# Sorted tables read eight entries at a time into the registers of four engines, in a routed matmul kernel

## The reference

```python
def _L0_cond_ref(x, cat_ids, W, b):
    selected_W = W[cat_ids]          # W: [32, 512, 512]
    selected_b = b[cat_ids]          # b: [32, 512]
    return jnp.einsum('bti,bio->bto', x, selected_W) + selected_b[:, None, :]
x = x + _L0_cond_ref(x, itok_B_0_30, L0_cond_W, L0_cond_b)   # x: [128, 128, 512] f32
```

## Time and profile before

| what | value |
|---|---|
| median of three runs | 361.69 us |
| the profiled execution's own time | 361.52 us |
| its span in the trace | 359.0 us |
| TensorE busy, share of the span | 99% |
| GpSimd, VectorE, ScalarE busy | 75%, 48%, 41% |
| register loads (L146): SyncE, TensorE, VectorE, GpSimd | 64, 32, 32, 7 |

### The profile page before, as it was taken

The page is one execution under the profiler, slowest core; times in us unless marked ns, Lnnn a source line. Parts: engine busy times, 40 slices in busy tenths (PEclk is TensorE's granted clock), DMA queues, the critical chain, the costliest instruction groups (busy, mean ns, idle before and its releaser), DMA issues.

```text
span 359.0 us, 6838 instructions
## 1 busy us (share of the span) xinstructions
PE 354.1 (99%) x1553; PEld 289.6 (81%) x1553; DVE 172.9 (48%) x277; ACT 146.9 (41%) x263; POOL 269.3 (75%) x147
## 2 busy tenths in 40 slices
PE   8999999999999999999999999999999999999996
PEld 3888888888888888888888888888888888888884
DVE  7665445444544544544454454454545445445442
ACT  5464344434433443443443343342544344334420
POOL 4788999997747698799965999799979799934000
PEclk9999999999999999999999999999999999999999
DMA  7999998999788988989997899989997999855632
GB/s 267 271 403 377 394 375 289 334 361 354 284 281 276 370 325 302 307 273 392 333 306 272 287 387 322 302 306 370 332 324 267 379 371 310 315 204 179 194 117 88
DMA packets 43668, 109.49 MB, mean 305 GB/s; under 512 B 4849, under 2 KB 4850, under 8 KB 39026
## 3 DMA queue, kind: packets, MB, share of 16 engines
q1 hardware_dynamic: 38018, 69.75, 54.3%
q0 software_dynamic: 5328, 38.28, 30.9%
q10 hardware_dynamic: 288, 1.05, 0.8%
HBM read 75.50 MB, written 33.55 MB: 304 GB/s over the span
## 4 chain that ended last, share of the span: by engine, by line
PE 98%; DVE 1%; issue 0%
PE pA L411 97%; PE pA L371 1%; DVE os L364 0%; DVE cmp L318 0%; DVE below L323 0%; DVE rank L320 0%; DVE hot L321 0%; PE pS L384 0%; DVE fill L305 0%; DVE colf L316 0%; PE pS L379 0%; DVE unit L307 0%; PE pS L378 0%; DVE num L322 0%; DVE ones L306 0%
## 5 line engine op out<-in xcount | busy, mean ns | idle before, releaser
L364 DVE TENSOR_TENSOR os<-pA,bb 128x512 f32<-128x512 f32 x128 | 88.5, 691 | 171.1 <-PE pA L411 169.2
L284 ACT ACTIVATE xh<-xs 128x512 fp32r<-128x512 f32 x127 | 80.4, 633 | 195.3 <-PE pA L411 133.2
L258 POOL TENSOR_TENSOR wl<-wr,wh 128x2048 fp32r<-128x2048 f32 x30 | 138.7, 4623 | 2.5
L411 PE MATMUL pA<-wh,xh 128*128 x512 | 137.2, 389 | 0.0
L411 PE MATMUL pA<-wl,xh 128*128 x512 | 137.0, 389 | 0.0
L411 PE MATMUL pA<-wh,xl 128*128 x512 | 136.9, 389 | 0.0
L411 PEld LDWEIGHTS pA<-wh,xl 128*128 128x128 f32 x512 | 96.0, 188 | 20.2 <-DVE xl L331 0.3
L411 PEld LDWEIGHTS pA<-wl,xh 128*128 128x128 f32 x512 | 96.1, 188 | 20.0
L411 PEld LDWEIGHTS pA<-wh,xh 128*128 128x128 f32 x512 | 96.0, 188 | 20.1
L336 DVE TENSOR_TENSOR xl<-pT,xh 128x512 fp32r<-128x512 f32 x127 | 86.6, 682 | 9.9 <-ACT pT L287 9.9
L254 POOL TENSOR_SCALAR wh<-wr 128x2048 fp32r<-128x2048 f32 x30 | 57.5, 1915 | 36.7 <-PE pA L411 34.9
(11 more groups left out here) (40 smaller groups left out, 13.3 us busy)
## 6 DMA issues: line engine op xcount, KB each, us to landing
xs<-xt SPq DMA_DIRECT2D x128, 256.0 KB, 5.3
out<-os SPq DMA_DIRECT2D x128, 256.0 KB, 5.0
wr<-w POOLq DMA_DIRECT2D x29, 1024.0 KB, 7.0
bb<-bias POOLq DMA_DIRECT2D x7, 1024.0 KB, 9.6
wr<-w ACTq DMA_DIRECT2D x2, 512.0 KB, 4.3
wr<-w SPq DMA_DIRECT2D x2, 512.0 KB, 5.7
wr<-w SPq DMA_DIRECT2D x4, 256.0 KB, 7.2
bb<-bias SPq DMA_DIRECT2D x2, 256.0 KB, 6.8
```

The costliest lines, as they stand in the source:

```text
L258: eng.tensor_tensor(wl[:, at], wr[:, c % NR, :], wh[:, at].bitcast(f32), ALU.subtract).then_inc(s_wp if c == 2 else s_w, 1)
L284: eng.activation(xh[:, i % NH, :, :], xs[:, i % NX, :, :], ACT.Copy).then_inc(s_xh, 1)
L364: eng.tensor_tensor(os[:, i % NO, :], pA[i % NA][:, :], bb[:, bass.ds(at, D)], ALU.add)._wait_ge(s_mm, i + 2).then_inc(s_fin, 1)
L411: mm = eng.matmul(pA[i % NA][:, :], xp[:, i % NH, k, :], wp[:, bass.ds(at + k * D, D)], start=(n == 0), stop=(n == 3 * KT - 1))
```

## The change

The default of `ahead` in `table` goes from 4 to 8, for all five users:

```diff
-        def table(eng, name, src, n, lo, hi, ahead=4):
+        def table(eng, name, src, n, lo, hi, ahead=8):
```

## The result

The changed kernel takes 360.90 us (median of 22 executions), the kernel before 361.71 beside it (22 executions). The interval lies clear of 1, so this is a small gain and not "no change".

What follows compares the result with a forecast made beforehand. The prediction took TensorE's unbroken piece of matmuls to bound the kernel. The profiled 361.52 us plus three terms of 0 gave 361.52, put at 361.65 between that and the runs' median of 361.69; range 361.3 to 362.2.

Steps and rivals of the forecast that it cites:

- What bounds the kernel: Whole span: TensorE's one piece of 1,536 matmuls, 348.36 us; only changing its length or start changes the time.
- TensorE in the steady part: TensorE's later loads: hidden under matmuls already queued, 3.6 us ahead; removing 16 loads gives 0.
- How long a load of eight takes: Register loads on all queues: extra time over a load of four, taken as 0.04 us, at most 0.33.
- D: What a load of eight entries takes beyond one of four: 0.04 us taken, 0.30 (SyncE) to 0.33 (TensorE) as upper bound.
- TensorE at the start: First load ahead of three filler matmuls, cover about 0.09 us: cost between 0 and 0.24 us, taken as 0.
- SyncE at the start: SyncE's early issues: from the fifth batch's fetch on, 0.30 - D earlier, 0.26 us; cost and gain 0.
- D near 0.6: Batch 9's inputs: the wait for class 1's second half would decide only once D is near 0.6.
- The sum: Whole time: profiled 361.52 us (span 359.0 and 2.5 around it) plus three zeros; 361.65 put as forecast.
- The doubled load: Rival: D = 0.33, TensorE starts 0.1 to 0.24 us late, time 361.75 to 361.9; 15 of the 88 in 100.
- "Two of four": Rival: a load of eight is carried out as two loads of four, time the same; no separate chance given.
- The late start that costs pace: Rival: array stands still between the early fillers, quicker matmul pace comes later, time 362.6 to 363; 4 in 100.
- "Loads do cost TensorE": Rival: the 16 removed loads had held up the array, time falls by up to 5.3 us to 356.2; 3 in 100.

Runs made afterwards that it cites:

- f3_tensor_by_5: The kernel before the change with TensorE's table read five entries at a time, 6 TensorE instructions fewer; 360.98 us, ratio 0.9979.
- f1_eight_plus_16_loads: The changed kernel with 16 loads of one entry added on TensorE, so its instruction count is as before the change; 361.87 us, ratio 1.0004.
- e1_tensor_only: The kernel before the change with only TensorE's table read eight entries at a time, the other users still four; 360.84 us, ratio 0.9978.
- e4_before_again: The kernel before the change, unchanged, run again; 361.58 us, ratio 0.9994.
- g3_after_again: The changed kernel, unaltered, run again beside the last group of experiments; 360.86 us, ratio 0.9978 against the kernel before.
- g1_first_of_four: The changed kernel with the first load of every table kept at four entries, all later ones eight; 360.82 us, ratio 0.9975 against the kernel before.
- e2_all_but_tensor: The changed kernel with TensorE's table back at four entries, SyncE, VectorE and GpSimd at eight; 361.83 us, ratio 1.0004 against the kernel before.

## Why the prediction was wrong, point by point

- *What bounds the kernel.* Right: the chain is 348.39 us of matmuls, and nothing that the change did to the queues is seen in it.
- *TensorE in the steady part, cost 0.* Right. Batch 8's load took 0.606 us at 25.4 and its first matmul began at 29.25, and even loads of 1.5 us (f3_tensor_by_5) stay hidden.
- *How long a load of eight takes, D = 0.04 us.* Wrong. It is 0.23 on SyncE, 0.25 on VectorE and 0.26 for TensorE's first load, near the upper bound of 0.30 to 0.33; by the medians of all TensorE's loads it is 0.47, above that bound, but under cover. The step that failed is the line drawn from one entry to four: between those the price is flat, as I had it (0.302 to 0.332), but it isn't flat beyond four. By 0.2 us for each register ("Runtime: NRT & Kernel Launch", section Instruction fetch mechanics, in the Trainium skill) four entries would be 0.8 and one 0.2, and the rows have 0.33 and 0.30. That page speaks of registers loaded from HBM; these tables lie in SBUF, and its figure does not describe their loads.
- *TensorE at the start.* The first filler's weight load came 0.26 later, as D says. The cover of 0.09 us was worked out from fillers 0.45 us apart, and that holds for some executions only: the array stood still for 0.42 us in the changed kernel, where the two fillers were done at 6.20, for 0.24 in f1_eight_plus_16_loads and for 0.04 in e1_tensor_only, all three with a first load of 0.77 to 0.78 us. The start was late by only 0.05 us against the profiled execution of the kernel before because that one had its fillers further apart. The kernel before in e4_before_again had them as close as the changed kernel, and there its matmuls begin at 7.12, 0.31 us sooner than at 7.43; yet its last matmul ends at 355.79, and that of g3_after_again, which begins at 7.43, at 355.78. So a later start of about this size is there, and batch 0 takes it back, as the prediction allowed with its 0.34 us of waits. g1_first_of_four, without the longer first load, has a median span of 359.0 against 359.1.
- *SyncE at the start.* Right in kind: 0.10 us sooner for the fifth batch against the 0.30 - 0.23 = 0.07 of the formula. Behind it the four loads of class 2's weights took 3.69 us to issue in this execution, so the sixth batch's fetch was at 13.19, later than before, and GpSimd's own fetch at 20.95 against 20.78. L263's wait still ended at 31.04 us, and batch 9 began in step at 31.74. The "D near 0.6" there is a slip: the bias landing (20.48 + D) and the path through class 1's second half (19.87 + D) move by the same D, so by this reckoning the second never decides.
- *The sum.* This is the step that decided. I wrote "span 359.0 and 2.5 around it" and carried the 2.5 over unasked. It was the one term that moved: 1.75 to 1.80 in its place, -0.77 us in the profiled executions. I had listed removed instructions only by the time that they take on their queues, and not by where they leave the end of TensorE's program against its blocks of 16 KB. That the tail holds TensorE's fetch, and that the gain goes with the place of the border, is shown by e1 to f3; how long the fetch itself holds the end up was not measured apart from the 0.8 us. Its share of 16 engines, 1.0% of 5.8 us, makes 0.9 us from its start to its landing, an estimate.
- *Rivals.* None of them was the answer. The doubled load came nearly true as a load, and its price was below a tenth of a microsecond. "Two of four" fits the shortest loads of eight, 0.59 us against 0.33, and has a price of its own. The late start that costs pace exists in some executions, up to 1.5 us longer, also of the kernel before; that of e2_all_but_tensor has no gap at the load, so a gap isn't needed for it, and whether one makes it more frequent is open. "Loads do cost TensorE" would have been faster for another reason and by up to 5.3 us.

The Trainium skill bears on this in the same section: it says that instructions are refilled in blocks of 16 KiB, 256 instructions, and that crossing a border is mostly hidden. The trace agrees on the size for TensorE, 17 packets and 0.28 MB on queue 8, but not for SyncE's queue 14, whose packets are 8 KB, and it agrees on "mostly": 17 fetches in the span left no gap in the chain. The one behind the span is the exception, and cost 0.8 us.

## What to carry to other kernels

When a change adds or removes instructions on an engine, look at the DMA view behind the end of the span, and at the time outside it: an instruction block fetched there is part of the measured time, and a few instructions more or fewer can put it in or out, here 0.8 us for 6 of them or fewer. Such a gain belongs to the length of the program and not to the edit, so it is neither a reason for the edit nor sure to outlive the next one; it takes an experiment that puts the count back to tell the two apart. A cost read at two sizes (one and four entries) says nothing on a third beyond both.

## What was not expected of the hardware

- An execution ends 0.8 us sooner when TensorE's last 16 KB instruction block is not fetched behind the span: 1.74 to 1.85 us outside the span with no such block, 2.3 to 3.1 with one in all but a few executions. SyncE's 8 KB block, which moves 0.6 us earlier, costs nothing that the medians show.
- A register load costs 0.30 us for one entry, 0.33 for four, 0.80 for eight and 1.55 for sixteen on TensorE, in the medians. Five cost 0.59 to 0.85 where the load begins at a multiple of four and 1.29 to 2.18 where it doesn't.
- Executions differ in when the quicker pace of matmuls begins, at a granted clock of 1.00 throughout, and a late one has a span 1.5 us longer: the changed kernel's profiled execution has two fillers in 0.54 us from 5.66 on, the one before still 0.45 us for each at 6.33, and that of e1_tensor_only comes to its pace near 10.4.
